# Causal zeros for the diagonal score tiles: GpSimd selects behind the exponential instead of mask products on TensorE

## Time and profile before

| | us |
|---|---|
| median of 3 runs | 907.96 (907.43 to 909.16) |
| the profiled execution's own time | 905.11 |
| its span | 903.3 |
| PE, DVE, POOL, ACT busy | 832.7, 605.4, 503.7, 493.2 |

### The profile page before, as it was taken

How to read it: one execution, slowest core, us unless ns; L and a number is a source line. 1 busy time by engine, 2 the same in 40 slices (tenths; PEclk the granted TensorE clock), 3 DMA queues, 4 the chain that set the end, 5 groups by cost and what they waited for, 6 DMA issues and landing times.

```text
span 903.3 us, 17582 instructions
## 1 busy us (share of the span) xinstructions
PE 832.7 (92%) x5281; PEld 455.9 (50%) x5282; DVE 605.4 (67%) x1187; ACT 493.2 (55%) x1214; POOL 503.7 (56%) x651
## 2 busy tenths in 40 slices
PE   5799986798989999989999999998999999999997
PEld 2365644233343433478888888873344343433444
DVE  2577776878886788755555555556788777888322
ACT  3465533154656557634444444446676766667662
POOL 3556650399889730056666666527878888800000
PEclk9799988789999999999999999998999999999999
DMA  7015544610000141048777778774585554500011
GB/s 224 1 44 175 184 159 155 174 53 19 1 19 2 37 108 33 1 126 240 223 224 241 236 229 240 135 140 70 73 172 90 73 88 71 90 12 1 13 36 48
DMA packets 81987, 96.15 MB, mean 106 GB/s; under 512 B 13031, under 2 KB 73447, under 8 KB 81895
## 3 DMA queue, kind: packets, MB, share of 16 engines
q0 software_dynamic: 19968, 31.47, 19.3%
q1 hardware_dynamic: 45033, 46.80, 17.2%
q10 hardware_dynamic: 16896, 16.78, 5.5%
HBM read 61.11 MB, written 33.82 MB: 105 GB/s over the span
## 4 chain that ended last, share of the span: by engine, by line
PE 78%; DVE 12%; issue 4%; DMA 2%; DVEq 1%; ACT 1%; POOLq 1%; POOL 1%; ACTq 0%; SPq 0%
PE bank L1199 14%; PE bank L1182 13%; PE vector_banks L1276 12%; PE vector_banks L1158 11%; DVE mpart L956 8%; PE vector_banks L1050 6%; PE bank L1289 6%; PE vector_banks L1071 4%; PE bank L1071 3%; PE bank L1050 2%; DMA xn_all<-wexp 2%; PE vector_banks L1219 2%; PE bank L1087 1%; PE vector_banks L1161 1%; PE bank L1185 1%
## 5 line engine op out<-in xcount | busy, mean ns | idle before, releaser
L956 DVE TENSOR_REDUCE mpart<-vector_banks 128x2 f32<-128x1024 f32 (+3 forms) x320 | 330.1, 1062 | 89.5 <-PE vector_banks L1158 50.6
L711 ACT ACTIVATE probs<-bank 128x512 f32<-128x512 f32 (+3 forms) x428 | 212.3, 538 | 132.5 <-PE bank L1182 65.0
L1182 PE MATMUL bank<-turned 99*128 99x512 bf16 (+3 forms) x640 | 202.7, 355 | 10.9 <-ACT probs L711 4.3
L1158 PE MATMUL vector_banks<-turned 96*128 96x512 bf16 (+3 forms) x640 | 185.9, 360 | 13.0 <-DVE mpart L956 12.2
L588 POOL DMA_INDIRECT turned<-normed_rows,tok_i x128 | 125.2, 978 | 124.7 <-PE vector_banks L1050 88.7
L603 POOL DMA_INDIRECT res<-expert_rows,slot_i x96 | 148.8, 1550 | 40.8 <-issue 28.7
L711 ACT ACTIVATE at_first<-bank 128x512 f32<-128x512 f32 (+3 forms) x212 | 105.8, 533 | 73.1 <-PE bank L1185 39.1
L1182 PEld LDWEIGHTS bank<-turned 99*128 99x128 bf16 x640 | 58.5, 98 | 168.8 <-ACT probs L711 74.7
L1276 PE MATMUL vector_banks<-xn_all,probs 128*128 x512 | 136.1, 389 | 2.9 <-DMA xn_all<-wexp 1.0
L1199 PE MATMUL bank<-probs,V 128*32 128x512 f32 (+3 forms) x856 | 102.5, 550 | 0.0
L1276 PEld LDWEIGHTS vector_banks<-xn_all,probs 128*128 128x128 f32 x512 | 87.9, 192 | 15.0 <-issue 6.9
(11 more groups left out here) (154 smaller groups left out, 967.5 us busy)
## 6 DMA issues: line engine op xcount, KB each, us to landing
expert_rows<-probs ACTq DMA_DIRECT2D x32, 512.0 KB, 4.3
term_rows<-at_first SPq DMA_DIRECT2D x96, 128.0 KB
turned<-term_rows SPq DMA_DIRECT2D x32, 384.0 KB, 4.6
xn_all<-wexp SPq DMA_DIRECT2D x32, 384.0 KB
normed_rows<-xn_all SPq DMA_DIRECT2D x4, 512.0 KB, 5.7
turned<-normed_rows,tok_i POOLq DMA_INDIRECT x128, 4.0
out<-res SPq DMA_DIRECT2D x16, 128.0 KB, 1.7
res<-x SPq DMA_DIRECT2D x1, 1536.0 KB, 8.4
```

Of the source, the lines that this page charges most:

```text
L711: A(PT[v // 2 % 6][:, v % 2, 0:width], bank[A_BANK[step][0]][:, 0:width], ACT.Exp).then_inc(s["scalar_bank_read"], 1)
L956: V.tensor_reduce(mpart[:, t % TPC, 2 * j:2 * j + 2, p], ring[:, :, 0:w], AX.X, ALU.max).then_inc(s["vector_bank_read"], 1)
L1158: last = mm(ring[:, h, 0:w], q_turned(slice(0, KQ), 2 * j + h, t * P, P), k_turned(par, slice(0, KQ), 2 * j + h, p * CH, w), start=True, s ...
L1182: last = mm(ring[:, 0:CH - off], k_turned(parity(g), slice(0, KM), h, kb * P, P), q_turned(slice(0, KM), h, c * CH + off, CH - off), start ...
```

## The change

For each diagonal block two new POOL steps, `mk`, stand in the order: behind the second and behind the fourth `st`. Each waits for the exponential of head 1 (or 3), then sets zeros in the first 128 columns of two heads' probabilities where the key is later than the query (a select over 128 partitions x 2 x 128 fp32), 128 selects in all. `pv` of a diagonal block also waits for the second. `mask_k`, its making and the 256 products go; `mask_q` with its products stays. The other POOL work is put into the same order by due times: the one-hot pairs from block 1 to 46 (96), the first 8 row gathers from block 57 to 62, the 96 sums from block 66 to 136. `tok` moves from blocks 8 to 50 to blocks 11 to 57.

```diff
-TOKENS_FROM, TOKENS_TO = 8, 50
+TOKENS_FROM, TOKENS_TO = 11, 57
+HOT_FROM, HOT_TO = 1, 46
+ROWS_FROM, ROWS_TO = 57, 62
+SUMS_FROM, SUMS_TO = 66, 136
...
+    fills = [[scores, score_goals, 0], [tokens, token_goals, 0], [ends, end_goals, 0],
+             [hots, hot_goals, 0], [first_rows, row_goals, 0], [sums, sum_goals, 0]]
...
         order.append(("st", g, c, kb, 1))
+        if kb >= TPC * c:
+            order.append(("mk", g, c, kb, 0))
         some()
...
         order.append(("st", g, c, kb, 3))
+        if kb >= TPC * c:
+            order.append(("mk", g, c, kb, 1))
         some()
...
-            gp.memset(mask_k[:, :], 0.0)
...
-            gp.affine_select(out=mask_k[:, :], in_=mask_k[:, :], compare_op=ALU.is_ge, fill=MASKED, base=0,
-                             pattern=[[1, P]], channel_multiplier=-1)
...
+                    elif step[0] == "mk":
+                        _, g, c, kb, j = step
+                        gp.wait_ge(s["scalar_bank_read"], A_AT["st", g, c, kb, 2 * j + 1] + 1)
+                        tile = PT[(2 * PV_AT["pv", g, c, kb] + j) % 6][:, :, 0:P]
+                        gp.affine_select(out=tile, in_=tile, compare_op=ALU.is_ge, fill=0.0, base=0,
+                                         pattern=[[0, 2], [1, P]], channel_multiplier=-1).then_inc(s["masked"], 1)
+                    elif step[0] == "rows":
+                        n = step[1]
+                        if n == 0:
+                            gp.wait_ge(s["xn_stored"], 16 * 4)
+                            gp.wait_ge(s["weights_stored"], 16 * 4)
+                            gp.wait_ge(s["tok_ready"], 1)
+                            gp.wait_ge(s["plan_ready"], 1)
+                        fetch_rows(n)
+                    elif step[0] == "sum":
+                        _, t, j = step
+                        if t >= AHEAD or j:
+                            gp.wait_ge(combined[t % AHEAD], 16 * (TOPK * (t // AHEAD) + j))
+                        gp.indirect_dma_start(res[:, t, :], None, yg_dram,
+                                              bass.IndirectOffsetOnAxis(ap=slot_i[:, t, j:j + 1], axis=0),
+                                              compute_op=ALU.add).then_inc(combined[t % AHEAD], 16)
...
-                        diag = kb >= TPC * c
                         last = mm(ring[:, 0:CH - off], k_turned(parity(g), slice(0, KM), h, kb * P, P),
-                                  q_turned(slice(0, KM), h, c * CH + off, CH - off), start=True, stop=not diag)
-                        if diag:
-                            last = mm(ring[:, 0:P], identb[:, :], mask_k[:, :], start=False, stop=True)
+                                  q_turned(slice(0, KM), h, c * CH + off, CH - off), start=True, stop=True)
...
                         pe.wait_ge(s["scalar_bank_read"], A_AT["st", g, c, kb, HG - 1] + 1)
+                        if kb >= TPC * c:
+                            pe.wait_ge(s["masked"], MK_AT["mk", g, c, kb, 1] + 1)
```

More of the change, by code:

```diff
@@ L115, in whole_order @@
     end_goals = [(0, 0), (4 * PROJECT_FROM, 0), (4 * (len(key_blocks) - 1), len(ends))]
+    hots = [("hot", t, j) for t in range(NT) for j in range(TOPK)]
+    hot_goals = [(0, 0), (4 * HOT_FROM, 0), (4 * HOT_TO, len(hots))]
+    first_rows = [("rows", n) for n in range(XR)]
+    row_goals = [(0, 0), (4 * ROWS_FROM, 0), (4 * ROWS_TO, XR)]
+    sums = [("sum", t, j) for t4 in range(0, NT, AHEAD) for j in range(TOPK) for t in range(t4, t4 + AHEAD)]
+    sum_goals = [(0, 0), (4 * SUMS_FROM, 0), (4 * SUMS_TO, len(sums))]
     chain = [("route", i) for i in range(ROUTE_PIECES)]
@@ L124, in whole_order @@
     order += [("mc", 0, 0), ("mt", 0, 0)]
-    fills = [[scores, score_goals, 0], [tokens, token_goals, 0], [ends, end_goals, 0]]
+    fills = [[scores, score_goals, 0], [tokens, token_goals, 0], [ends, end_goals, 0],
+             [hots, hot_goals, 0], [first_rows, row_goals, 0], [sums, sum_goals, 0]]
     later = []
@@ L226, in layer @@
     MC_AT = places(order, lambda step: step[0] == "mc")
+    MK_AT = places(order, lambda step: step[0] == "mk")
     with ExitStack() as ctx:
@@ L363, in layer @@
         mask_q = sb("mask_q", [P, P], BF16)
-        mask_k = sb("mask_k", [P, P], BF16)
         mpart = sb("mpart", [P, TPC, HG, NCH])
@@ L388, in layer @@
             vector_bank_full vector_bank_read scalar_bank_full scalar_bank_read
-            v4_ready mcat_ready pv_done o_read
+            masked v4_ready mcat_ready pv_done o_read
             exp_x_psum exp_x_ready gu_done gate_ready exp_h_ready exp_hT_psum exp_hT_ready y_done y_read weights_in written""".split()
@@ L562, in _ @@
             split_terms(NT - 1, (NT - 1) % 2)
[L564 to L576, removed]
+            def fetch_rows(n):
+                gp.indirect_dma_start(xg[:, n % XR, :], None, xn_dram,
+                                      bass.IndirectOffsetOnAxis(ap=tok_i[:, n:n + 1], axis=0)).then_inc(rows_in[n % XR], 16)
+            def attend(steps):
+                for step in steps:
+                    if step[0] == "hot":
+                        _, t, j = step
+                        if t == 0 and j == 0:
+                            gp.wait_ge(s["slots_ready"], 1)
+                        if t >= HOT and j == 0:
+                            gp.wait_ge(s["vector_bank_full"], D_AT["tok", (t - HOT) // 2] + 1)
+                        gp.tensor_scalar(lo_hot[t % HOT][:, j, :], count_from_1[:, :], lo1[:, t, j:j + 1], None, ALU.is_equal)
+                        last = gp.tensor_scalar(hi_hot[t % HOT][:, j, :], count_from_0[:, :], hi[:, t, j:j + 1],
+                                                token[:, t:t + 1], ALU.is_equal, ALU.mult)
+                        if j == TOPK - 1:
+                            last.then_inc(s["hot_made"], 1)
+                    elif step[0] == "mk":
[13 more added lines that the diff above has]
+                    elif step[0] == "sum":
+                        _, t, j = step
+                        if t >= AHEAD or j:
[3 more added lines that the diff above has]
+                                              compute_op=ALU.add).then_inc(combined[t % AHEAD], 16)
@@ L578, in take_weights @@
+            attend(early)
             def take_weights(n):
@@ L587, in _ @@
                     gp.wait_ge(s["slot_w_made"], n - XR + 1)
-                gp.indirect_dma_start(xg[:, n % XR, :], None, xn_dram,
-                                      bass.IndirectOffsetOnAxis(ap=tok_i[:, n:n + 1], axis=0)).then_inc(rows_in[n % XR], 16)
+                    fetch_rows(n)
                 if n >= 3:
@@ L596, in _ @@
             gp.wait_ge(s["shared_added"], NT)
[L598 to L608, removed]
+            attend(late)
         @block.scalar
```

## The result

Slower: 919.4 us, median of four runs (916.4 to 921.0), against 908.6 (907.4 to 912.7) for the kernel before, run beside it. The ratio is 1.0115, 95% interval 1.0089 to 1.014. Forecast were 903.7 and a range of 899 to 911.5. The profiled execution took 916.44 us (span 914.5), 11.3 more than the profiled one of before.

What follows compares the result with a forecast made beforehand. The prediction took PE as the bound late (busy 270 of 279 us), early only in part. Terms: -11.6 gain + 11.8 lateness - 4.5 absorbed = -4.3 us, giving 903.7 us against the median; range 899 to 911.5.

Steps and rivals of the forecast that it cites:

- Gain, 11.6 us: PE, diagonal blocks: removing the 256 mask products saves their share of the chain, 7.5 us late and 4.1 us early.
- A select's price, 0.35 apart, 0.40 long: POOL: a 256-column select takes 0.40 us, 0.35 us between starts, estimated from 128-column selects and POOL's slope per column.
- the first rival: POOL becomes the bound in diagonal runs; selects at the upper bound of 0.49 us apart give 912.7 us; chance 0.25.
- A sum among selects 1.70: POOL, late stage: a sum with selects around it counts 1.55 + 0.15 = 1.70 us.
- Lateness, 11.8 us: PE's `pv` waits for selects queued on POOL, mostly in runs of diagonal blocks: 11.8 us in all.
- bare ends: The last block and block 63, where `pv` closely follows its exponential: 0.55 us each, 1.1 us together.
- The 2.0 "under way": A sum or pair may be running on POOL when a diagonal run begins: 2.0 us for the runs together.
- 4.5 us absorbed by DVE's lead: Three runs of eight diagonal blocks: PE runs ahead of DVE, so 1.5 us of stall in each costs nothing.
- The sign that had been named for this: If DVE still holds its 3.54 us at two late places although PE stalled just before, nothing was absorbed.
- The second rival: DVE absorbs none of the lateness, so saving and waits cancel: 908.2 us, no change; chance 0.16, with other ways to cancel.
- The clock, chance 0.02: PE falls to half clock behind late `pv`: about 3.4 us each, 17 us over five runs, 920 us; chance 0.02.
- Moved at no cost: Moving `tok`, row gathers, weight copies and sums to later places in the order costs nothing.

Runs made afterwards that it cites:

- both_lighter: Changed kernel with sums and one-hot pairs thinned in diagonal blocks, first weight copies behind their gathers: 898.1 us, 0.9927 of the kernel before; again 901.2 us, 0.9955.
- changed_again: The changed kernel run once more, unaltered: 916.0 us, 1.0109 of the kernel before.
- pairs_lighter: Changed kernel with one-hot pairs at half rate in diagonal blocks from block 36, list to block 50, `tok` to 59: 912.9 us, 1.010 of the kernel before.
- sums_lighter: Changed kernel with the 96 sums spread from block 65 to 148, at half rate in diagonal blocks: 905.0 us, 1.0012 of the kernel before.
- masks_back: Changed kernel's layout of POOL work, but without selects and with the mask products back on PE: 907.8 us, 1.003 of the kernel before.
- lighter_lists_masks_on_pe: Layout of both_lighter with early weight copies, but mask products on PE and no selects: 906.8 us, 1.000 of the kernel before.
- select_per_head: Changed kernel with each select of 2 x 128 columns split into two of 128: 921.5 us, 1.0187 of the kernel before.

## Why the prediction was wrong

The forecast was -4.3 us; measured are +10.8. Step by step:

- **Gain, 11.6 us.** Mis-sized. Late 7.5 became 7.0 and 5.2 in the two layouts, and the 7.0 holds some 2 us of another cause (blocks 64 to 84, above). Early 4.1 became 2.2 and 2.3. The time shows 6.8 us (4.3 to 9.2) for the products alone. A product's share of the chain was taken for what its removal gives. Early, where DVE's maxima held 18.9% of the chain, PE probably just waited longer for DVE; no run separates that.
- **A select's price, 0.35 apart, 0.40 long.** Right to within 0.04 us: 0.36 to 0.39 apart, and 0.41 long. The estimate from POOL's slope held, so the first rival's price, 0.445 or more, did not come. Its picture did, POOL without idle time in the diagonal runs, but the forecast's own price was enough for it. By the 1.5 ns an element that the "GPSIMD Engine Reference" of the Trainium skill (Performance versus the Vector engine) has for a best case, the estimate had been 0.57 us; the measurement decides against that figure for this operation. What the same section of the Trainium skill says against GpSimd for elementwise work compares it with VectorE; no run here put the selects on VectorE, so none bears on it. Against products on TensorE the selects lost as the change was laid out and won in both_lighter.
- **A sum among selects 1.70.** 1.77. A pair with a select: 1.37 + 0.35 = 1.72; 1.72 measured.
- **Lateness, 11.8 us.** Right in sum, 11.5, and nearly by place. Each wait of PE for a select, after: run to block 43 3.0 us (2.21, .52, .27; forecast 2.9), run to 83 3.0 (.10, 1.09, 1.80; 1.5), run to 123 3.4 (.39, .10, 1.09, 1.80; 3.2), runs of four .50 each (.25), bare ends .36 and .48 (.55 each), first pairs .30 (.6). The 2.0 "under way" are in these. The list of waits puts one more, .50 at 205.74 in block 10, down to a select, but it stands in front of an `mx` product, which by the program waits for DVE and for no select.
- **4.5 us absorbed by DVE's lead.** This is the step that failed. Nothing was: 1.80 us of wait cost 2.0 in changed_again, 7.2 us of waits 9.0 between pairs_lighter and sums_lighter, and the 2.21 at block 42's `pv` came with 3.5 us more for the four blocks behind it. A chain that stands on DVE (3.54 us) was read as PE being ahead and able to wait; that piece, from 672.99, also begins before the late `pv` (673.97) and not behind it, as the prediction had it. But the `mx` products that DVE needs stand in PE's own order behind the late `pv`; when PE stops, DVE runs dry (1.86 and 2.31 us idle, above), and then both are late. The sign that had been named for this, DVE still holding its 3.54 us, did not come: late, the chain of the kernel after has no piece of DVE's maxima over 1.23 us, and POOL's sums hold 16.8% of it. The second rival had the missing absorption right; its time, 908.2, lacked what follows.
- **The clock, chance 0.02.** The second failure. It fell behind three of the five large waits, for 3.4, 3.4 and 6.8 us. The blocks 124 to 128 show its price alone, 1.9 us for 6.8. For 13.6 us at half clock that makes 3.7 us, and half of 13.6, 6.8, is the most it can be. The argument against had been that waits of up to 1.7 us do not do what one of 2.73 us did. No row supported that limit: 1.80 us sufficed, though not each time. The trace of before could have warned of it. Near the start of its early stage, where PE has other gaps close by, a wait of 1.74 us for DVE is followed by half clock (PE in order of time, then by stretch):

```profile
152.93 2.76 PE L1240 MATMUL bank<-at_first,onesb 128*128 128x480 bf16 x15 [1.74 <-DVE at_first L894]
...
153.60:157.00 3.40, 3.40 (x18) 2.02 (x17) 0.00 (x0) 0.49 (x1) 0.00 (x0) 0.50 0.54 190
```

- **Moved at no cost.** True within 0.6% by masks_back and 0.3% by lighter_lists_masks_on_pe. The experts' 2.9 us more were put at nothing here; what makes them isn't settled, and one profiled execution of each kernel is little to tell them from scatter.

The terms by the profiles: -9.2 (7.0 late, 2.2 early) + 11.5 of waits + 3.7 to 6.8 of half clock + 2.9 of experts = 8.9 to 12.0; with the gain of the new layout, 7.5, it is 10.6 to 13.7. Measured 11.3 between the two profiled executions. With the lateness all paid, the forecast's own terms give 908.2; the clock, the smaller gain and the experts are what leads from there out of the range.

## What to carry to other kernels

An engine at 61% may have no time at all in the stretch where the new work arrives; work moved to it must come with a schedule of its other work that leaves room in that stretch, and both_lighter shows that the schedule, not the operation, decides the sign. A lead of one engine over another absorbed no stall here, since what feeds the second stands in the first one's queue behind the stall: look for that before counting on a lead. And a stall on PE is priced with what the clock may do behind it.

## What the runs showed of the hardware

- PE's granted clock fell to its lower level behind waits of 1.80 us (for a select) and 1.66 us (for DVE) in a stage in which it had been 0.99 on average, and stayed there 3.4 or 6.8 us. The same wait at the same place left it at 1.00 in another execution of the same kernel, and both waits of 1.80 us left it there in pairs_lighter. In select_per_head one of 2.04 us (start at 687.06) left it at 1.00 and one of 1.34 (799.00) had 3.4 us at half clock with it. So the length of the wait alone doesn't fix whether it falls.
- A select of 128 x 2 x 128 fp32 with a strided pattern: 0.41 us long, 0.36 to 0.39 to the next start. A select of 128 columns takes 0.24 to 0.25 (bf16) or 0.26 (fp32, select_per_head, two in 0.52), so the second 128 columns cost some 0.1 to 0.15.
- A POOL instruction behind an indirect DMA is shown as 1.00 us long (0.41 elsewhere) and starts 0.97 us after the DMA's own start, inside its 1.55 us. A sum alone takes 1.85 us from start to start, with a select behind it 2.13: so the first select there costs 0.28.
